# Tile numbers loaded into registers without stated bounds, in a graph network kernel with attention and a router

## What is computed

```
edge_index = jnp.stack([src, dst])
xn = _layernorm(x, axis=-1)
x = x + _L0_gnn_ref(xn, edge_index, ...) + _L0_mix_ref(xn[None], ...)[0]
x = x + _L0_ffn_ref(_layernorm(x, axis=-1)[None], ...)[0]
```

```
rows, cols = (edge_index[0], edge_index[1])
q = (embeds[rows] @ qT).reshape(-1, HEAD, hd)
k = (embeds[cols] @ kT).reshape(-1, HEAD, hd)
v = (embeds[cols] @ vT).reshape(-1, HEAD, hd)
att = jnp.clip(jnp.einsum('ehd,ehd->eh', q, k), -10.0, 10.0)
expAtt = jnp.exp(att)
attNorm = jax.ops.segment_sum(expAtt, rows, num_segments=n)[rows]
res = (expAtt / (attNorm + 1e-08))[..., None] * v
out = jax.ops.segment_sum(res, rows, num_segments=n) + embeds
```

## Time and profile before

| what | value |
|---|---|
| runs | 9469.74, 9429.08, 9467.54 us; median 9467.54 |
| the profiled execution, first to last instruction | 9471.2 us |
| VectorE (DVE) busy | 5826.3 us, 62% |
| PE busy | 5314.8 us, 56% |
| GpSimd (POOL) busy | 5179.6 us, 55% |
| ScalarE (ACT) busy | 1019.5 us, 11% |
| instructions | 116748 |

### The profile page before, as it was taken

The page is one execution under the profiler, slowest core; times in us unless marked ns, Lnnn a source line. Parts: engine busy times, 40 slices in busy tenths (PEclk is TensorE's granted clock), DMA queues, the critical chain, the costliest instruction groups (busy, mean ns, idle before and its releaser), DMA issues. The chain is left out here.

```text
span 9471.2 us, 116748 instructions
## 1 busy us (share of the span) xinstructions
PE 5314.8 (56%) x27325; PEld 4169.2 (44%) x27325; DVE 5826.3 (62%) x15897; ACT 1019.5 (11%) x3273; POOL 5179.6 (55%) x5420
## 2 busy tenths in 40 slices
PE   6868555555455555455555555555657777776331
PEld 3545444444444444344444444444535555554220
DVE  7878445555555555666666666666745555555776
ACT  0000100000000000100000000000212222221220
POOL 2323156666666666366666666666155555555762
PEclk6555777777776777777777777777668888887555
DMA  1000333333333333333333333333322222222325
GB/s 27 3 7 3 78 108 106 110 104 109 104 109 104 109 109 107 91 100 100 100 100 101 100 100 99 102 100 102 102 42 47 49 47 50 47 50 50 88 67 154
DMA packets 504090, 777.84 MB, mean 82 GB/s; under 512 B 121545, under 2 KB 364222, under 8 KB 503442
## 3 DMA queue, kind: packets, MB, share of 16 engines
q0 software_dynamic: 202656, 454.22, 18.2%
q1 hardware_dynamic: 292838, 304.95, 12.0%
q10 hardware_dynamic: 7948, 11.21, 0.5%
HBM read 698.60 MB, written 71.36 MB: 81 GB/s over the span
## 5 line engine op out<-in xcount | busy, mean ns | idle before, releaser
L676 POOL DMA_INDIRECT att_kv_e<-kv,gnn_idx x3336 | 3396.0, 1018 | 2151.2 <-DVE att_vals L796 1012.2
L748 PE MATMUL att_ps_sum<-att_vals,att_hot 128*125 128x136 f32 x6672 | 1317.4, 356 | 2323.8 <-DVE att_vals L796 1971.6
L748 PEld LDWEIGHTS att_ps_sum<-att_vals,att_hot 128*125 128x125 f32 x6672 | 1131.0, 246 | 2528.0 <-DVE att_vals L796 2115.8
L676 POOL DMA_INDIRECT max_rows<-rows,gat_idx x1128 | 1064.5, 944 | 951.3 <-ACT src_sb L1806 442.9
L737 PE MATMUL att_ps_q<-qs,att_hot_t 125*128 x6672 | 1294.5, 336 | 239.2 <-issue 226.8
L813 DVE TENSOR_TENSOR acc<-acc,att_ps_sum 125x136 f32 x1668 | 488.4, 293 | 1322.7 <-DMA rows<-sort_zeros 950.0
L737 PEld LDWEIGHTS att_ps_q<-qs,att_hot_t 125*128 125x128 f32 x6672 | 1135.3, 244 | 318.7 <-issue 314.7
L1826 DVE CUSTOM_DVE_ANT_0 max_junk<-max_far,max_ps_b 125x256 bf16<-125x256 bf16 x2256 | 803.2, 417 | 511.9 <-PE max_ps_b L1792 266.7
L772 DVE TENSOR_TENSOR att_prod<-att_ps_q,att_kv_e 128x512 f32<-128x512 f32 x834 | 569.0, 682 | 875.5 <-remote 799.0
L759 ACT ACTIVATE att_vals<-att_clipped 128x32 f32<-128x32 f32 x834 | 191.3, 229 | 4935.1 <-DVE att_clipped L804 2161.9
L1792 PE MATMUL max_ps_b<-max_a_t,pick_head 12*125 12x512 bf16 x1128 | 380.1, 461 | 464.6 <-ACT max_a_t L1801 427.4
(11 more groups left out here) (445 smaller groups left out, 7124.3 us busy)
## 6 DMA issues: line engine op xcount, KB each, us to landing
att_local<-gnn_loc_rows SPq DMA_DIRECT2D x834, 128.0 KB
att_kv_e<-kv,gnn_idx POOLq DMA_INDIRECT x3336
max_local<-gat_loc_rows SPq DMA_DIRECT2D x282, 128.0 KB
gs_local<-gat_loc_rows SPq DMA_DIRECT2D x141, 256.0 KB, 3.2
outs<-ex_y SPq DMA_DIRECT2D x25, 896.0 KB
max_rows<-rows,gat_idx POOLq DMA_INDIRECT x1128
ans_late<-outs SPq DMA_DIRECT2D x11, 896.0 KB
ans_early<-outs SPq DMA_DIRECT2D x8, 896.0 KB
```

The costliest lines, as they stand in the source:

```text
L676: pool.indirect_dma_start(rows(j, e), None, source, bass.IndirectOffsetOnAxis(ap=g.idx[:, t:t + 1], axis=0))\
L748: ins = pe.matmul(ps_sum[j % 2][0:NODE_TILE, p * 256:p * 256 + SUMS], hot[:, j, PAIR * p + e, :], vals[:, j % 2, PAIR * p + e, :], start=e ...
```

## The change

`value_load` is no longer given the range of the number. With a range, it puts behind the load a compare of the register with 0 and 49 and an assert on its result, and then nothing more is checked. Without one, each instruction that addresses a tensor by the register gets the check: the compare and an assert at the first access, and one more assert at each further access of the same number (an add that reads and writes its tile has two accesses, a pair of matmuls too). All of them are register instructions in the queue of the engine. The lines behind L1836 move up by one.

```diff
 def attend(...):                      # both attention layers
         def node_tile(eng, pair):
-            return eng.value_load(tile_of[0:1, bass.ds(pair, 1)], min_val=0, max_val=g.tiles - 1)
+            return eng.value_load(tile_of[0:1, bass.ds(pair, 1)])
...
 def neighbour_max(...):               # the router's first pass
-                    t = dve.value_load(tile_of[0:1, bass.ds(k * (GROUP // PAIR) + p, 1)], min_val=0,
-                                       max_val=g.tiles - 1)
+                    t = dve.value_load(tile_of[0:1, bass.ds(k * (GROUP // PAIR) + p, 1)])
...
 def neighbour_sum(...):               # the router's second pass
         def node_tile(eng, pair):
-            return eng.value_load(tile_of[0:1, bass.ds(pair, 1)], min_val=0, max_val=g.tiles - 1)
+            return eng.value_load(tile_of[0:1, bass.ds(pair, 1)])
```

## The result

| | median of 4 runs | lowest to highest |
|---|---|---|
| before | 9468.64 us | 9429.08 to 9470.89 |
| after | 9610.67 us | 9590.39 to 9653.50 |

The ratio is 1.0165, with a 95% interval of 1.0146 to 1.0185: the change costs 142 us between the medians, 156 by the ratio and 138 to 175 by the interval. The forecast was 9575 in a range of 9480 to 9690, with 0.69 on slower. The profiled execution of the changed kernel is the longest of its four, 43 us above their median, so its stretches together overstate the change.

What follows compares the result with a forecast made beforehand. VectorE's instruction stream was taken to pace the router's second pass, GpSimd's gathers attention, with VectorE on the path only in windows. 41 + 62 + 5 = 108 us on 9471.2, less 4, gives 9575 us; range 9480 to 9690.

Steps and rivals of the forecast that it cites:

- Second pass, 41 us: Router's second pass on VectorE: 4 more asserts per step at 0.073 us, times 141 steps, 41 us; bounds 25 to 60.
- The walk along the step: Router's second pass: L2025 about 0.5 us earlier, next adds +0.3, +0.4 and some 0.05; net +0.2 to +0.3 us a step.
- Attention on VectorE, 62 us: Both attention layers: moved checks cost 249 us raw on VectorE, of which 0.25 is on the path, 62 us.
- The share of time that gathers wait for VectorE, 0.19: Attention: GpSimd's gathers wait 1012.2 of 5367 us for `att_vals`; used as low-end weight on the raw cost, 47 us.
- The slope of 0.42 from the two layers: Attention: elapsed time differs between layers by 0.42 us per us of VectorE work; the high end, 105 us.
- The low bound: Attention on VectorE: hidden steps cost nothing outside windows; some 70 windows with 0.15 us each, 10 us.
- PE, 0: Attention and router's second pass: PE's added checks hide under its waits, zero; uncovered, 117 us and up to 200 us.
- First pass, 5 us: Router's first pass: 110 us raw on VectorE, but gathers wait for ScalarE and VectorE idles; 5 us, between 0 and 28.
- Attention pays fully: Rival: in attention fewer steps pass per window and windows multiply; 105 to 249 us, typical total 9650; chance 0.15.
- Only the second pass pays: Rival: attention absorbs it all, only the router's second pass pays; 51 us in all, 9518 us; chance 0.2.
- The queue hides everything: Rival: asserts and moved compares find cover in each place, no change, 9467 us; chance 0.07.
- Faster: Rival: second pass gains 63 us from loads without compares (9404 us), or attention has fewer windows; chance of both 0.08.

## Why the forecast held, and where its terms were off

The time fell into the range, a third of the way from the forecast to its upper bound, and the sign and the mechanism (checks exposed behind the waits, paid in the second pass by VectorE's stream and in attention through the windows) were borne out. The terms were not equally good, and that the total came as near owes something to luck: the second pass was put too high, attention and the first pass too low, and the windows on which attention's term rests are absent in four of the seven series.

*Second pass, 41 us.* It is 28 by four pairs of stretches and 36 and 33 by medians; at the low end of 25 to 60. The walk along the step was right: 0.5 us gained ahead of L2025, 0.27 and 0.35 lost ahead of the next two adds (0.3 and 0.4 were forecast), the net +0.2 us a step (28.5 / 141) that stood in it. The error was to take the plain product 4 x 0.073 x 141 and not the result of the walk. The price of an assert, 0.073, measured 0.06: the 0.20 us between the instructions had been shared out evenly, 0.05 each, while 0.034 us stand ahead of an assert.

*Attention on VectorE, 62 us.* This is the term that was mis-sized. The raw cost was 210 and not 249. One reason is a miscount: where the queue was already exposed the order shows one new assert between the adds and not two, so they stand 0.83 apart in a window and not 0.92. But 96 us by medians and 122 by the first pair of stretches came out of it, a share of 0.46 to 0.58 where 0.25 had been taken. The share of time that gathers wait for VectorE, 0.19, was the wrong weight: a slower step makes the windows more and longer. The slope of 0.42 from the two layers would have given 88 for 210 us, near the 96; it was discounted for PE's sake, and PE's part shows nothing. The low bound counted some 70 windows, which no row gives; the trace of before has 87 over 2 us in layer 1 and 103 in layer 2.

*PE, 0.* Nothing without windows, in both stages; with windows nothing that shows beside the scatter.

*First pass, 5 us.* 28 and 21 us in two pairs of traces with windows, at the upper bound; 3, which is not told from 0, without. That the gathers there wait for ScalarE's `src_sb` 442.9 us was taken as cover. Whether the 28 and 21 belong to the change stays open: no run changed the first pass alone with windows, and the waits in it vary by more between series. VectorE's waits ahead of its custom maxima (L1826) with the releaser "remote", which stood for PE's late signals in attention, are 107.0 us before and 323.2 in the changed kernel, but 639.6 with VectorE's attention changed alone, where this pass is as before; without windows there are none.

*The rivals.* "Attention pays fully" had as its mechanism that fewer steps pass per window and the windows multiply, which is what layer 1 shows; its typical time of 9650 lies above the 9611 measured, while the 96 to 122 us of attention lie about its low end of 105. "Only the second pass pays" is what happens without windows: 8156 against 8120 for the second pass alone, and attention alone at 0. "The queue hides everything" fell everywhere, since the second add of a pair moved from 0.43 to 0.77 us in every trace with VectorE's change in attention; without windows its time came true for attention, not because the queue hid it but because the gathers set the pace. "Faster" had the gain ahead of L2025 right and its return behind it too small. The number of GpSimd's waits for VectorE moved by 14, inside the 20 allowed, and their total by 144.5 us. The chances as listed (0.50, 0.15 and half of 0.20) add up to 0.75 for slower by more than half a per cent and not to 0.69; nothing else rests on it.

## What to carry to other kernels

A bounds check costs what stands behind the last wait before its use: read from the order whether compare and assert lie ahead of the wait or behind it, and price those behind it (0.06 us for an assert and 0.22 for a compare here). An engine that is idle half of the time is not thereby off the path: count how many steps pass between two stalls and how long a stall is, and ask whether a slower step makes the stalls more or longer. Where the data's origin guarantees the range, stating the range without a run-time check was worth more here (152, 146 and 341 us) than either placement.

## What the runs showed of the hardware

The same program has two levels of time that last for a whole series of runs: 8090 to 8120 us in four series and 9455 to 9556 in three (9468 in the first). It is no property of a chip, since one chip showed 9556 in one series and 8107 in a later one. Within a series the runs of before agree within 0.5%. The difference lies in the gathering stages: the second pass takes 568 to 569 us at both levels. It goes with PE's signals reaching VectorE late, 10.6 us in the middle after the recorded matmul where VectorE waits for one; in a window the first signal comes 2.1 us in the middle after GpSimd's last gather has ended (0.9 to 2.5 in eight of ten). One gather takes as long at both levels (1.00 to 1.04 us on the mean of a layer with windows, 1.00 to 1.02 without), so slower gathers are not the cause; what delays the signals stays open. It matters for reading any result here: attention's part of this change is 0 at one level and some 100 us at the other.

In the second pass PE's busy time goes from 176 to 268 us for the same 2208 matmuls at the same granted clock of 0.50, at no cost in time. It is the work of PE's own register instructions: 268 in the kernel with PE alone changed, 173 in the one with VectorE alone. A fetch matmul (L1980) takes 197 ns in place of 184 on the mean, but with an assert between two of them they no longer overlap, and together they cover 148.0 us in place of 52.5. VectorE's `gs_hot_t` takes 0.48 us in the changed kernel (9052.27 above) and 0.73 in the kernel before, `gs_hot` 1.32 and 1.20, for the same shapes, and GpSimd's busy time falls from 387 to 282 us for as many instructions. These go with VectorE's change and not with PE's (GpSimd 282 and 387 us in the two kernels that separate them); why is open.
